# The last group of a fused attention and feed-forward kernel gets a feed-forward program of its own, and the scale spreads become transposes

## What is computed

```python
x = x + xattn(layernorm(x), ctx)        # 16 heads of 64; 124 context tokens, and 4 more with weights of their own; low-rank parts added to the weights
x = x + ffn(layernorm(x))

def ffn(x):                              # hidden width 1024
    h = bit_linear(x, w1)                # rows rounded to 8-bit levels by their own largest value, weights ternary
    h = silu(depthwise_conv1d(h, conv_w, conv_b))   # three taps along the tokens, within a sequence
    return bit_linear(h, w2)
```

## Time and profile before

| | |
|---|---|
| time, median of 3 runs | 1571.66 us (1570.80 to 1572.26) |
| profiled execution, its own time | 1570.99 us |
| its span | 1569.0 us |
| TensorE matmul busy | 1441.2 us (92%), 10778 instructions |
| VectorE / ScalarE / GpSimd busy | 1214.9 us (77%) / 1177.5 us (75%) / 660.0 us (42%) |
| mean granted TensorE clock | 0.975 |

### The profile page before, as it was taken

The page is one execution under the profiler, slowest core; times in us unless marked ns, Lnnn a source line. Parts: engine busy times, 40 slices in busy tenths (PEclk is TensorE's granted clock), DMA queues, the critical chain, the costliest instruction groups (busy, mean ns, idle before and its releaser), DMA issues.

```text
span 1569.0 us, 33374 instructions
## 1 busy us (share of the span) xinstructions
PE 1441.2 (92%) x10778; PEld 1174.6 (75%) x10778; DVE 1214.9 (77%) x3059; ACT 1177.5 (75%) x3909; POOL 660.0 (42%) x1058
## 2 busy tenths in 40 slices
PE   7899999999999999999999999999999999998743
PEld 4688788787878878787877878787887878787621
DVE  4364797887879798787969888786978878786966
ACT  3487887968778796978878797887879787787721
POOL 2354444434444443445344444444444344444500
PEclk9999999999999999999999999999999999999965
DMA  9100001000000100000010100000010100000000
GB/s 280 44 30 27 19 15 45 15 29 14 28 29 14 43 14 31 13 28 29 18 38 14 43 0 28 29 28 29 14 43 9 34 14 28 29 1 28 1 14 13
DMA packets 41128, 47.13 MB, mean 30 GB/s; under 512 B 3008, under 2 KB 35200, under 8 KB 41088
## 3 DMA queue, kind: packets, MB, share of 16 engines
q1 hardware_dynamic: 41088, 46.62, 9.8%
HBM read 36.13 MB, written 10.49 MB: 30 GB/s over the span
## 4 chain that ended last, share of the span: by engine, by line
PE 52%; ACT 20%; DVE 19%; issue 9%; DMA 0%; DVEq 0%; ACTq 0%; POOL 0%; SPq 0%; POOLq 0%
PE PS L478 10%; ACT SM L675 8%; PE PS L440 8%; PE PS L491 6%; PE PS L421 5%; PE PS L456 5%; PE PS L465 4%; PE PS L430 4%; PE PS L539 4%; ACT HP L696 2%; DVE GBS L887 2%; PE PS L518 2%; DVE GBS L908 2%; ACT GBS L701 2%; ACT QM L642 2%
## 5 line engine op out<-in xcount | busy, mean ns | idle before, releaser
L1053 POOL TENSOR_TENSOR SM<-SM,RC 128x496 f32<-128x496 f32 (+1 forms) x512 | 331.6, 668 | 747.8 <-DVE RC L822 742.1
L675 ACT ACTIVATE SM<-PS,MX 128x124 f32<-128x124 f32 x1024 | 358.7, 366 | 147.9 <-DVE SM L828 145.8
L478 PE MATMUL PS<-KT,QM 128*128 128x128 f32 x2048 | 278.2, 279 | 29.3 <-ACT SM L675 29.2
L478 PEld LDWEIGHTS PS<-KT,QM 128*128 128x128 f32 x2048 | 249.4, 192 | 44.8 <-ACT SM L675 44.5
L675 ACT ACTIVATION_READ_ACCUMULATOR SM<-PS,MX 128x1 f32 x1024 | 212.9, 208 | 0.0
L1084 POOL TENSOR_TENSOR OTl<-OF,OTh 128x256 fp32r<-128x256 f32 x256 | 196.0, 766 | 14.6 <-ACT OF L669 14.6
L667 ACT ACTIVATE OTh<-PS 128x256 fp32r<-128x256 f32 x256 | 100.4, 392 | 116.3 <-PE PS L456 115.1
L465 PE MATMUL PS<-IDF,SM 128*128 128x128 f32 x1024 | 168.4, 287 | 8.1 <-POOL SM L1053 8.0
L826 DVE TENSOR_REDUCE MX<-PS 128x4 f32<-128x496 f32 x256 | 170.1, 664 | 0.2 <-issue 0.2
L456 PE MATMUL PS<-PT,V 128*64 128x128 f32 x2048 | 168.8, 286 | 0.1
L456 PEld LDWEIGHTS PS<-PT,V 128*64 128x64 f32 x2048 | 106.8, 136 | 81.9 <-issue 74.9
(11 more groups left out here) (142 smaller groups left out, 3566.4 us busy)
## 6 DMA issues: line engine op xcount, KB each, us to landing
XIN<-in_x SPq DMA_DIRECT2D x16, 512.0 KB, 3.6
XRES<-in_x SPq DMA_DIRECT2D x16, 512.0 KB, 3.6
out_y<-HP SPq DMA_DIRECT2D x16, 512.0 KB, 3.0
CRAW<-in_ctxT SPq DMA_DIRECT2D x16, 256.0 KB, 2.7
RRAW<-in_ctxT SPq DMA_DIRECT2D x32, 128.0 KB, 2.9
QM<-in_Wq SPq DMA_DIRECT2D x1, 1024.0 KB, 9.4
GBS<-in_Wo SPq DMA_DIRECT2D x1, 1024.0 KB, 14.1
k_ipa_columns<-HP SPq DMA_DIRECT2D x1, 1024.0 KB, 6.6
```

The costliest lines, as they stand in the source:

```text
L478: m = mm(psS[:, h, :], QM[:, 2 * q + h // 2, h % 2, TOK * b:TOK * b + TOK], KT[:, 2 * q + h // 2, b, :], start=True, stop=True)
L675: m = act.activation(SM[s % 2][:, h, 0:ORG], psS[:, h, 0:ORG], ACT.Exp, bias=MX[s % 2][:, h:h + 1], accum_out=SU[s % 2][:, h:h + 1])
L1053: m = pool.tensor_tensor(part, part, RC[c % 2][:, 4 * i:4 * i + 4].unsqueeze(2).broadcast_to(shape), ALU.mult)
```

## The change

1. A function `finish_last` on TensorE and on VectorE replaces `finish` for group 15. Both halves of X2 and the statistics stand ahead of the first output half of group 14; the normalised rows and Q1 go to XIN and CRAW, which are free by then; the first spread has bank 3 to itself and no longer waits for Q1T; the first layer's products rotate through five banks (5, 0, 1, 2, 7); each quarter of the channel maxima is transposed when it is there; the second layer runs tile by tile over both halves in banks 0 and 1; the output is stored in two parts.
2. In the half steps behind the last attention group ("drain"), ScalarE's copies of the last chunk stand ahead of group 14's L686, and its output projection ahead of group 14's second layer.
3. In all groups, both spreads are `pe.transpose` of the same broadcast column in place of a product with the identity.

```diff
@@ -78,6 +78,7 @@
+L_X2, L_NORM, L_QT, L_F2 = (4, 5), 7, 13, M_HMAX + 8
...
@@ -215,6 +226,12 @@
+
+        F1_BANKS = [PS[:, i, :] for i in (5, 0, 1, 2, 7)]
+        last_q1t, last_bc = PS[:, 6, :], PS[:, 3, :]
+        last_f2 = [PS[:, c, :] for c in range(2)]
+        last_xn2 = XIN
+        last_q1 = CRAW[:].bitcast(BF16).rearrange("p (b d) -> p b d", d=DM)
...
@@ -338,7 +355,11 @@
             def finish(g, n):
-                if n == FINISH_HALVES - 1:
+                if is_last(g) and n == FINISH_HALVES - 1:
+                    for c in range(2):
+                        sp.wait_ge(fin_done, g.count(2, c + 1))
+                        sp.dma_start(seqs(out, g)[:, 2 * c:2 * c + 2, :], OUTT[:, 2 * c:2 * c + 2, :]).then_inc(out_done, 16)
+                elif n == FINISH_HALVES - 1:
                     sp.wait_ge(fin_done, g.count(2, 2))
                     sp.dma_start(seqs(out, g), OUTT).then_inc(out_done, 16)
 
...
@@ -493,7 +514,58 @@
+            def finish_last(g, n):
+                if n == L_QT:
+                    pe.wait_ge(scale_done, g.count(2, 1))
+                    for b in range(NB):
+                        m = pe.transpose(last_bc[:, TOK * b:TOK * b + TOK], AD[0][:, b:b + 1].broadcast_to([P, P]), IDF[:])
+                    m.then_inc(bc_full, 1)
+                    pe.wait_ge(q1_done, g.count(1, 1))
+                    pe.wait_ge(unit_free[1], g.count(UNITS // 2, UNITS // 2))
+                    bank = last_q1t.bitcast(BF16).rearrange("p (k b t) -> p k b t", k=2, b=NB)
+                    for k in range(2):
+                        for b in range(NB):
+                            m = pe.transpose(bank[:, k, b, :], last_q1[:, b, P * k:P * k + P], IDB[:])
+                    m.then_inc(q1t_full, 1)
+                j = tile_at(n - M_F1)
+                if 0 <= j < CT:
+                    if j == 0:
+                        pe.wait_ge(q1t_done, g.count(1, 1))
+                        pe.wait_ge(unit_free[0], g.count(UNITS // 2, UNITS // 2))
+                        pe.wait_ge(s_used, g.count(CHUNKS, CHUNKS))
+                        pe.wait_ge(pt_done, g.count(CHUNKS, CHUNKS))
+                        pe.wait_ge(ot_high, g.count(CHUNKS, CHUNKS))
+                        pe.wait_ge(fin_done, g.count(2, 0))
+                    if j >= len(F1_BANKS):
+                        pe.wait_ge(g_done, g.count(CT, j + 1 - len(F1_BANKS)))
+                    for k in range(2):
+                        m = mm(F1_BANKS[j % len(F1_BANKS)], W1[:, k, P * j:P * j + P], Q1T[:, k, :], start=(k == 0), stop=(k == 1))
+                    m.then_inc(f1_full, 1)
+                if n == M_HT:
+                    for b in range(NB):
+                        pe.wait_ge(hm_done, g.count(NB, b + 1))
+                        m = pe.transpose(psF[:, TOK * b:TOK * b + TOK], HM[:, b, :], IDF[:])
+                    m.then_inc(ht_full, 1)
+                if n == M_BC2:
+                    pe.wait_ge(scale_done, g.count(2, 2))
+                    for b in range(NB):
+                        m = pe.transpose(last_bc[:, TOK * b:TOK * b + TOK], AS[1][:, b:b + 1].broadcast_to([P, P]), IDF[:])
+                    m.then_inc(bc_full, 1)
+                if n == L_F2:
+                    for j in range(CT):
+                        pe.wait_ge(q2_done, g.count(CT, j + 1))
+                        for c in range(2):
+                            for b in range(2):
+                                tok = slice(TOK * (2 * c + b), TOK * (2 * c + b) + TOK)
+                                m = mm(last_f2[c][:, DM * b:DM * b + DM], Q2[j][:, tok], W2[:, j, :],
+                                       start=(j == 0 and b == 0), stop=(j == CT - 1), skip_group_check=True)
+                            if j == CT - 1:
+                                m.then_inc(f2_full, 1)
+
             def finish(g, n):
...
@@ -506,7 +578,7 @@
                     for b in range(NB):
-                        m = mm(psF[:, TOK * b:TOK * b + TOK], AD[0][:, b:b + 1].broadcast_to([P, P]), IDF[:], start=True, stop=True)
+                        m = pe.transpose(psF[:, TOK * b:TOK * b + TOK], AD[0][:, b:b + 1].broadcast_to([P, P]), IDF[:])
...
@@ -607,7 +679,10 @@
-                    project_out(g, n // 2)
+                    if not (is_drain(g) and n == 6):
+                        project_out(g, n // 2)
+                    if is_drain(g) and n == 4:
+                        project_out(g, 3)
                 if g.reg is None:
...
@@ -678,13 +753,18 @@
             def finish(g, n):
+                if n == L_QT and is_last(g):
+                    act.wait_ge(bc_full, g.count(2, 1))
+                    need(act, g_done, g.count(CT, 0))
+                    act.activation(BC[:], last_bc, ACT.Identity).then_inc(bc_done, 1)
                 if n == M_QT + 1:
                     act.wait_ge(q1t_full, g.count(1, 1))
-                    act.activation(Q1T[:].rearrange("p k t -> p (k t)"), psF.bitcast(BF16), ACT.Identity).then_inc(q1t_done, 1)
+                    bank = last_q1t if is_last(g) else psF
...
                     act.activation(OUTT, X2[:], ACT.Identity).then_inc(copy_done, 1)
-                if n == M_BC1 + 1:
+                if n == M_BC1 + 1 and not is_last(g):
...
@@ -736,8 +816,11 @@
             def steps(g, n):
+                if is_drain(g) and n == 3:
+                    output_copies(g, 2)
                 if n % 2 == 0:
-                    output_copies(g, n // 2)
+                    if not (is_drain(g) and n == 4):
...
@@ -828,7 +911,106 @@
+            def finish_last(g, n):
+                for c in range(2):
+                    if n == L_X2[c]:
...
+                        dve.tensor_tensor(X2[:, 2 * c:2 * c + 2, :], psY[c], XRES[:, 2 * c:2 * c + 2, :], ALU.add).then_inc(x2_done, 1)
+                if n == L_X2[1]:
+                    dve.wait_ge(x2_done, g.count(2, 2))
...
+                    variance(g, 1, ln2_stats, ln2_mv, ln2_var)
+                if n == L_NORM:
+                    dve.wait_ge(ln2_rstd, g.count(1, 1))
+                    normalise(1, last_xn2, X2).then_inc(ln2_done, 1)
...
+                    dve.tensor_reduce(AR[0][:], last_xn2[:], AX.X, ALU.max, apply_absolute_value=True).then_inc(quant[0], 1)
+                    scales(g, 0, CLIP, 127.0, 1.0 / 127.0)
+                    dve.wait_ge(scale_done, g.count(2, 1))
+                    for b in range(NB):
+                        m = dve.tensor_scalar(last_xn2[:, b, :], last_xn2[:, b, :], AS[0][:, b:b + 1], MAGIC, ALU.mult, ALU.add)
+                    m.then_inc(q1_scaled, 1)
+                    dve.wait_ge(q1_scaled, g.count(1, 1))
+                    dve.tensor_scalar(last_q1, last_xn2[:], MAGIC, None, ALU.subtract).then_inc(q1_done, 1)
+                j = tile_at(n - M_F1)
+                if 0 <= j < CT:
+                    dve.wait_ge(f1_full, g.count(CT, j + 1))
+                    if j == 0:
+                        dve.wait_ge(bc_done, g.count(1, 1))
+                    if j >= 4:
+                        dve.wait_ge(h_done, g.count(CT, j - 3))
+                    dve.tensor_tensor(GB[j % 4].rearrange("p b t -> p (b t)"), F1_BANKS[j % len(F1_BANKS)], BC[:],
+                                      ALU.mult).then_inc(g_done, 1)
+                j = tile_at(n - M_F1 - M_LAG[2])
+                if 0 <= j < CT:
+                    conv_next(g, j)
...
+                if n == M_Q2:
+                    dve.wait_ge(bc_full, g.count(2, 2))
+                    for k in range(CT // 2 + 1):
+                        if k < CT // 2:
+                            for j in range(2 * k, 2 * k + 2):
+                                if j >= 4:
+                                    dve.wait_ge(q2_done, g.count(CT, j - 3))
+                                dve.tensor_tensor(GB[j % 4].rearrange("p b t -> p (b t)"), HT[j], last_bc, ALU.mult).then_inc(q2_scaled, 1)
+                        if k > 0:
+                            dve.wait_ge(q2_scaled, g.count(CT, 2 * k))
+                            for j in range(2 * k - 2, 2 * k):
+                                dve.tensor_scalar(Q2[j], GB[j % 4].rearrange("p b t -> p (b t)"), MAGIC, MAGIC,
+                                                  ALU.add, ALU.subtract).then_inc(q2_done, 1)
+                if n == L_F2:
+                    for c in range(2):
+                        dve.wait_ge(f2_full, g.count(2, c + 1))
+                        if c == 0:
+                            dve.wait_ge(copy_done, g.count(1, 1))
+                        for b in range(2 * c, 2 * c + 2):
+                            m = dve.scalar_tensor_tensor(out=OUTT[:, b, :], in0=last_f2[c][:, DM * (b % 2):DM * (b % 2) + DM],
+                                                         scalar=AD[1][:, b:b + 1], in1=OUTT[:, b, :], op0=ALU.mult, op1=ALU.add)
+                        m.then_inc(fin_done, 1)
+
+            def conv_next(g, j):
...
```

(25 more changed lines are left out.)

47 lines of the change are left out of this document (35 added, 12 removed).

## The result

The changed kernel takes **1551.41 us** (median of four runs, 1550.24 to 1551.65), the kernel before took 1571.23 beside it: a ratio of 0.9872, 95% interval 0.9855 to 0.9889. The profiled execution took 1551.65 with a span of 1549.7, 19.3 less than the 1569.0 before. TensorE's matmuls are 10650 (1423.8 us) instead of 10778, its mean granted clock 0.983 instead of 0.975.

The account below looks back on a forecast made before the run. Predicted bound: in the loop VectorE's wait for the second spread, behind the attention group 15's FFN dependency chain. Terms summed to 19.95 us off 1570.99, giving 1551.0; the median 0.67 above makes 1551.7, range 1547.0 to 1556.0.

Parts of the forecast that it names:

- The loop: Groups 0 to 13: VectorE's wait for the second spread saves 0.15 us per group, 2.1 in all; the first spread saves nothing.
- The rival in which TensorE's 0.45 counts in full: Loop, second spread: TensorE's own time bounds it, 0.45 counts instead of 0.15, 4.2 us more, 1547.5; chance 0.12.
- the one in which the loop gives nothing: Loop and five banks both give nothing because VectorE bounds both, 2.1 + 2.2 us less, 1556.0; chance 0.12.
- Handover: Last group, up to its normalisation: X2 halves and statistics come earlier, normalisation at 1500.4 instead of 1504.55, gain 4.15 us.
- normalisation to first layer: Last group: 10.39 us from normalisation to first layer falls to 7.55, with the first spread beside the path; gain 2.84.
- clock at the transposes: Last group, ahead of the first layer: transposes come 4 us earlier, perhaps still at full clock; 0.4 us, bounds 0 and 0.85.
- I take a loss of 0.1, bounds 0 and 1.0.: Last group: first L696 overwrites OUTT and waits for group 14's store, issued about 1506.5, landing after 3.0 us.
- First layer, 2.2: Last group's first layer: VectorE idles 0.3 us where it idled 2.5, gain 2.2; VectorE is then the bound.
- The walk: First layer: new order stepped through with traced durations, each instruction starting when engine and inputs are there; gave 2.2 us.
- Second layer, 6.0: Last group's second layer, run by tile: 16.71 us before, end at 10.7 with the clock rising on its way; gain 6.0.
- Store, 0.2: Kernel end: last store part is 256 KB, landing in 2.7 us instead of 3.0 for 512 KB; 0.2, bounds 0 and 0.6.
- The price of a transpose: Both spreads: four transposes take 0.60 us by L523's row, against 1.05 for eight matmuls; the skill's rule would give 0.26.

Follow-up runs that it names:

- e2: The changed kernel with the spreads of groups 0 to 14 written as products again, the last group keeping its transposes; 1553.59 us.
- e8: e3 with the last attention chunk's output projection and its copy back at their old place, behind group 14's first second-layer half on TensorE; 1555.12 us.
- e12: The changed kernel with 16 unread products (32 instructions) added on TensorE between the last output projection and group 14's second layer; 1550.38 us.
- e3: The changed kernel with group 14's output added into and stored from XRES instead of OUTT, so the last group need not wait for that store; 1549.9 us.
- e9: e3 with its five banks, but VectorE scales each tile behind the convolution steps of the same place, as in the kernel before; 1552.66 us.
- e5: e3 with all the last group's first-layer products in one bank (7) instead of five; 1550.92 us.
- e6: e3 with the second layer waiting until all eight tiles are rounded before its first product; 1555.05 us.
- e4: The changed kernel with the last group's output in one store of 512 KB behind both halves; 1552.09 us.
- e10: The changed kernel measured once more, unaltered, on the same chip as e11; 1551.9 us.
- e11: e7 again, on the chip of e10; 1548.31 us, ratio to the kernel before 0.9858.
- e7: e3 with products whose result nobody reads in TensorE's idle places of the last group; 1549.28 us.

## Why the prediction was right

1551.7 was forecast, 1551.41 came. The sum was 0.65 too high against the profile. The two terms furthest off have opposite signs: the first layer with its store wait gave 1.65 less than taken, the last store 0.5 more. That the total came so close is in part luck.

- **The loop.** Right: 0.15 per group was taken, 0.17 came, and VectorE's own work, L876, now ends last. The rival in which TensorE's 0.45 counts in full is refuted by the period of 90.18, the one in which the loop gives nothing by e2. The step to group 14's L1081, 2.80 for 2.55, is a sum of 1.98 from the loop and 1.40 between group 12 and group 14, less a start that came 0.58 later; the 1.40 is more than the transposes explain and differs from profile to profile (see below).
- **Handover, normalisation to first layer, clock at the transposes.** Right within 0.12 each. Of the handover, e8 gives 3.80 to the new places of the last projection and its copies and 0.39 to VectorE's order. Full clock at the transposes (0.67 for L528, 1.03 before) was the 0.4; in e12 they took 0.93, so this term too depends on where the clock falls.
- **"I take a loss of 0.1, bounds 0 and 1.0."** This step failed: the store wait cost 1.76 in e3 against the changed kernel, outside the bounds. The store's issue was right: worked out 6.1 behind the normalisation (1500.4 to 1506.5), measured 1497.48 to 1503.58. What failed is the 3.0 to landing: it took 4.5. At 2.9 it is in time, as e12 shows. The median of 16 stores in the earlier trace rows was not the price of this store; the load of instructions beside it stood in no row of the prediction. The section's test, "a gap ahead of the first L696 ended by a DMA", was met.
- **First layer, 2.2.** The size was right (2.21 in e3), and VectorE is the bound, as "Five banks buy no more than this" goes on to say. The walk took the new order and the banks at once and did not part them. e9 and e5 do: the banks buy nothing without the order, the order buys 0.85 with one bank, and the banks 1.36 on top of it.
- **Second layer, 6.0.** 6.19. I had let the clock rise on the way; it rose after 1544, near the end. The closeness is in part luck: with the same second layer it took from 7.15 (e3) to 8.22 (e12) from the first product to the last store issue, for which the term would have been 6.7 to 5.6. e6 shows what the tile-by-tile start is worth by itself: 5.1. The Trainium skill (Perfetto Trace Analysis, Matmul Optimizations) has it that matmuls should execute back-to-back in batches, which speaks for the batch. Here the batch of 6.48 us had full clock only at its very end, and it lost, since it also had to wait for the last tile.
- **Store, 0.2.** 0.72 (e4: 0.7). The two prices in the earlier trace rows, 3.0 and 2.7, are of a store and of a load; a store of 256 KB takes 2.2.
- **The price of a transpose.** 0.60 per spread of four, and 1.11 at half clock, as the row of L523 had it. The 0.26 by the Trainium skill (TensorE: Matmul & The Clock Gate, Terms) did not show: the gain is that four instructions stand for eight.

What stays open: between group 12 and group 14 a profile spends up to 1.5 us more or less (from group 13's L908 or L1081 to group 14's: 80.55 before, 79.63 changed, 81.13 in e3, which has the same program there), in the stretch in which the granted clock dips. This program spends 79.6 there in the changed kernel, e4, e5, e10, e11 and e12 and 80.9 to 81.2 in e3 and e6 to e9, and e7 and e11 are one and the same kernel, so medians of different runs compare to about 1 us and the tails are the surer measure. What sets the depth of the dip was not tried, nor why the clock rises at 1541 in one run's second layer and at 1544 in another's. Not tested by a run of its own were the first spread off the path, the channel maxima's earlier transposes (0.65) and the new places in the handover without VectorE's new order; these are read from the two profiles alone.

## What to carry to other kernels

In a chain in which engines hand over to each other, the order on the engine that works most and the buffers go together: here the buffers gave nothing under the old order, the new order 0.85 with one buffer, and both 2.21. Let that engine do first what another engine waits for, then add the buffers that this order needs, and test each without the other. Before you take a difference from two traces, see that the record you count from is in both. If a transfer lands late, look into the DMA queues for what ran beside it, loads of instructions included, and don't price it by the median of its kind. Where TensorE starves beside a long vector stretch and is needed at once afterwards, products that nobody reads can be cheaper than a half-clock start (0.6 us here).

## What the runs showed of the hardware

- A load of instructions for an engine (0.02 MB on q8, 1.3 us of one DMA engine) made a store of 512 KB that ran beside it land in 4.2 to 5.2 us instead of 2.9. In e12, 32 more instructions of TensorE moved it by 6 us (1504.5 to 1498.0), and the store landed in 2.9 again.
- After TensorE had idled 7.65 us, 32 matmuls of 128x256 without a gap took 6.48 us and stayed at the 1.2 GHz level up to 1548 (e6: granted 0.50 in 1544 to 1548, 0.58 in 1548 to 1549). With 14 filler products ahead of them (5.99 us, granted 0.50 up to 1528), the four transposes of the channel maxima ran at the 2.4 GHz level, 0.33 each instead of 0.48 (e7: granted 1.00 in 1530 to 1535).
- Four transposes of 128x128 in float32 took 0.60 at full clock and 1.11 at half; the eight matmuls of the product that they replace took 1.05 and 2.08.
